# A ranking model on one core: VectorE places fetched rows, ScalarE fetches thirteen fields in one run, and the middle tiles take their rows in six groups

## The reference

```python
x0 = emb[ids].reshape(ids.shape[0], -1)
x = x0
for i in range(cross_w.shape[0]):
    s = x @ cross_w[i]
    x = x0 * s[:, None] + cross_b[i] + x
h = jax.nn.relu(x0 @ w1 + b1)
h = jax.nn.relu(h @ w2 + b2)
h = jax.nn.relu(h @ w3 + b3)
logit = jnp.concatenate([x, h], axis=1) @ out_w + out_b
return jax.nn.sigmoid(logit)
```

## Time and profile before

| | us |
|---|---|
| median of 3 runs (515.51 to 515.76) | 515.7 |
| profiled execution | 515.57 |
| its span, first to last instruction | 513.8 |
| TensorE busy | 478.8 (93%) |
| GpSimd busy | 372.1 (72%) |
| VectorE busy | 247.9 (48%) |
| ScalarE busy | 33.5 (7%) |

### The profile page before, as it was taken

How to read it: one execution, slowest core, us unless ns; L and a number is a source line. 1 busy time by engine, 2 the same in 40 slices (tenths; PEclk the granted TensorE clock), 3 DMA queues, 4 the chain that set the end, 5 groups by cost and what they waited for, 6 DMA issues and landing times.

```text
span 513.8 us, 13128 instructions
## 1 busy us (share of the span) xinstructions
PE 478.8 (93%) x2912; PEld 444.7 (87%) x2912; DVE 247.9 (48%) x490; ACT 33.5 (7%) x68; POOL 372.1 (72%) x400
## 2 busy tenths in 40 slices
PE   2699899998998999899899999999999899999997
PEld 1399798898998889899799989888898889999996
DVE  5776446354363635436264443645454263544335
ACT  4642000000000000000000000000000000000112
POOL 5777777777777777777777777777777777777740
PEclk9999999999999999999899999999999899999999
DMA  7981111111111111111111111111111111111100
GB/s 223 385 300 29 29 28 26 31 27 27 29 29 28 26 32 27 28 30 27 28 28 30 28 28 30 29 26 28 29 28 26 31 28 26 28 29 26 27 18 2
DMA packets 18142, 24.61 MB, mean 48 GB/s; under 512 B 7845, under 2 KB 8832, under 8 KB 18064
## 3 DMA queue, kind: packets, MB, share of 16 engines
q0 software_dynamic: 12576, 12.90, 11.3%
q1 hardware_dynamic: 4154, 9.71, 5.3%
q10 hardware_dynamic: 1334, 1.17, 0.7%
HBM read 24.41 MB, written 0.01 MB: 48 GB/s over the span
## 4 chain that ended last, share of the span: by engine, by line
PE 61%; POOL 18%; issue 11%; DMA 6%; DVE 3%; ACT 0%; POOLq 0%; DVEq 0%
PE l_bank L733 50%; POOL x_raw L345 18%; DMA x_raw<-in_L_rec_emb,idx 6%; PE x_bank L745 4%; PE x_bank L733 2%; PE h_bank L787 2%; DVE x_raw L510 2%; PE l_bank L818 1%; PE h_bank L757 1%; DMA ids<-in_r_ids 1%; PE h_bank L829 0%; PE l_bank L757 0%; DVE xT_lo L534 0%; PE h_bank L733 0%; DVE xT_hi L517 0%
## 5 line engine op out<-in xcount | busy, mean ns | idle before, releaser
L345 POOL DMA_INDIRECT x_raw<-in_L_rec_emb,idx x393 | 371.2, 945 | 122.2 <-issue 107.6
L733 PE MATMUL l_bank<-w_hi,xT_hi 128*128 128x342 f32 (+1 forms) x624 | 144.9, 333 | 0.1
L733 PE MATMUL l_bank<-w_lo,xT_hi 128*128 128x342 f32 (+1 forms) x624 | 138.5, 322 | 0.0
L733 PE MATMUL l_bank<-w_hi,xT_lo 128*128 128x342 f32 (+1 forms) x624 | 138.1, 321 | 0.0
L733 PEld LDWEIGHTS l_bank<-w_lo,xT_hi 128*128 128x128 f32 x624 | 107.3, 191 | 0.0
L733 PEld LDWEIGHTS l_bank<-w_hi,xT_hi 128*128 128x128 f32 x624 | 105.0, 192 | 2.6 <-DVE xT_lo L534 0.4
L733 PEld LDWEIGHTS l_bank<-w_hi,xT_lo 128*128 128x128 f32 x624 | 106.9, 191 | 0.0
L517 DVE CAST xT_hi<-x_bank 128x512 fp32r<-128x512 f32 (+2 forms) x56 | 33.1, 592 | 94.2 <-PE x_bank L745 94.2
L510 DVE COPY_PREDICATED x_raw<-past,x_bank 128x512 f32<-128x512 int32 (+1 forms) x66 | 40.3, 610 | 57.4 <-DMA x_raw<-in_L_rec_emb,idx 56.9
L745 PE MATMUL x_bank<-identity,x_raw 128*128 128x128 f32 x208 | 34.8, 280 | 17.0 <-DVE x_raw L510 16.9
L733 PE MATMUL l_bank<-w_hi,h1T_hi 128*128 128x512 f32 x120 | 48.7, 406 | 0.9 <-DVE h1T_lo L539 0.9
(11 more groups left out here) (97 smaller groups left out, 310.4 us busy)
## 6 DMA issues: line engine op xcount, KB each, us to landing
ids<-in_L_rec_emb SPq DMA_DIRECT2D x1664, 0.2 KB
ids<-in_L_rec_emb ACTq DMA_DIRECT2D x1280, 0.2 KB
w_raw<-in_L_rec_w SPq DMA_DIRECT2D x18, 512.0 KB, 14.6
x_raw<-in_L_rec_emb,idx POOLq DMA_INDIRECT x393, 2.4
b_rows<-in_L_rec_b ACTq DMA_DIRECT2D x1, 512.0 KB
b_rows<-in_L_rec_b ACTq DMA_DIRECT2D x1, 256.0 KB
ids<-in_r_ids SPq DMA_DIRECT2D x1, 208.0 KB, 2.6
b_rows<-in_L_rec_b ACTq DMA_DIRECT2D x1, 128.0 KB
```

Of the source, the lines that this page charges most:

```text
L345: pool.indirect_dma_start(out=dst, out_offset=None, in_=emb, in_offset=rows).then_inc(landed, 16)
L733: done = pe.matmul(bank[:, 0:b - a], x[:, k, :], w[:, k, a:b], start=(k == 0 and n == 0), stop=(k == last_k and n == 2))
```

## The change

- Tiles 1 to 14 take their chunks in six groups of 3, 2, 2, 2, 2 and 2; tile 0 keeps four groups, tile 15 its own six. Counters of groups follow (`seen`).
- VectorE copies the rows that were fetched one by one into place (`place`, ahead of the masked copy of the group that holds fields 20 and 21).
- ScalarE fetches field 20 of thirteen tiles instead of ten (tiles 2, 12 and 15 are new), in one run with loads of 32 addresses: 16 rows ahead of tile 0's last cast, the rest behind it, and all of them ahead of its work for tile 15. It stops only for a free one of its two buffers.
- VectorE takes over the casts of tile 0's first hidden layer, of tile 15's first two groups, and of the second hidden layer of tile 14; the cast and the subtraction of the second hidden layer stand one group later.

```diff
-    SIZES = [4, 3, 4, 2]
+    FIRST_GROUPS = in_groups([4, 3, 4, 2])
+    GROUPS = in_groups([3, 2, 2, 2, 2, 2])
...
-    ACT_TILES = [3, 4, 5, 6, 8, 9, 10, 11, 13, 14]
+    ACT_TILES = [2, 3, 4, 5, 6, 8, 9, 10, 11, 12, 13, 14, 15]
...
-    ACT_SHARES = [24, 28, 24, 28]
+    ACT_FIRST = 16
+    ACT_REGS = 32
...
             def first_step():
...
                     if g == 1:
                         load_rows()
+                    if g == len(FIRST_GROUPS) - 1:
+                        act.wait_ge(sp_idx_ready, 1)
+                        fetch(ACT_FIRST)
                     x_hi(0, g)
-                h1_hi(0)
...
+                fetch(ACT_REGS - ACT_FIRST)
+                while fetched[0] < P * len(ACT_TILES):
+                    fetch(ACT_REGS)
...
             def last_step(t):
-                x_hi(t, 0)
-                h2_hi(t - 1)
-                for g in range(1, len(LAST_GROUPS)):
+                for g in range(2, len(LAST_GROUPS)):
                     x_hi(t, g)
...
+            def place(t, g):
+                if t in SP_TILES and SP_FIELD // FPK in groups(t)[g]:
+                    i = SP_TILES.index(t)
+                    dve.wait_ge(sp_landed[i % SP_BUFS], 16 * P * (i // SP_BUFS + 1))
+                    dve.tensor_copy(x_buf[t % 2][:, SP_FIELD * E:(SP_FIELD + 1) * E], sp_rows[i % SP_BUFS]).then_inc(sp_placed, 1)
+                if t in ACT_TILES and ACT_FIELD // FPK in groups(t)[g]:
+                    j = ACT_TILES.index(t)
+                    dve.wait_ge(act_landed[j % ACT_BUFS], 16 * P * (j // ACT_BUFS + 1))
+                    dve.tensor_copy(x_buf[t % 2][:, ACT_FIELD * E:(ACT_FIELD + 1) * E], act_rows[j % ACT_BUFS]).then_inc(act_placed, 1)
+
             def make_whole(t, g):
+                place(t, g)
```

More of the change, by code:

```diff
@@ L24, in dcn_ranker_kernel, with in_groups @@
     FPK = P // E
-    SIZES = [4, 3, 4, 2]
-    NG = len(SIZES)
-    GROUPS = [list(range(sum(SIZES[:g]), sum(SIZES[:g + 1]))) for g in range(NG)]
-    assert sum(SIZES) == K1
+    def in_groups(sizes):
+        assert sum(sizes) == K1
+        return [list(range(sum(sizes[:g]), sum(sizes[:g + 1]))) for g in range(len(sizes))]
+    FIRST_GROUPS = in_groups([4, 3, 4, 2])
+    GROUPS = in_groups([3, 2, 2, 2, 2, 2])
     LAST_GROUPS = [[0, 1, 2, 3], [4, 5, 6], [7, 8], [12], [9, 10], [11]]
@@ L36, in groups, with seen @@
     def groups(t):
-        return LAST_GROUPS if t == TILES - 1 else GROUPS
-    FIRST = GROUPS[0][-1] * FPK + FPK
+        return LAST_GROUPS if t == TILES - 1 else FIRST_GROUPS if t == 0 else GROUPS
+    def seen(t):
+        return sum(len(groups(u)) for u in range(t))
+    NG = max(len(groups(t)) for t in range(TILES - 1))
+    assert all(len(groups(t)) % 2 == 0 for t in range(TILES))
+    FIRST = FIRST_GROUPS[0][-1] * FPK + FPK
     QUICK = 2
@@ L104, in dcn_ranker_kernel @@
     LO_READ = [5, 10, 13, 17]
-    assert all(HI_AHEAD[g].stop > max(COPIES - 1, GROUPS[g][0] - 1 + COPY_WITH - 1) for g in range(NG))
+    assert all(HI_AHEAD[g].stop > max(COPIES - 1, ks[0] - 1 + COPY_WITH - 1) for g, ks in enumerate(FIRST_GROUPS))
     ctx = ExitStack()
@@ L177, in dcn_ranker_kernel @@
         x_bank = [pb(f"x_bank{i}") for i in range(2)]
-        assert all(len(ks) * P <= 512 - E for t in (0, TILES - 1) for ks in groups(t)[1::2])
+        assert all(len(ks) * P <= 512 - E for t in range(TILES) for ks in groups(t)[1::2])
         end_bank = x_bank[1][:, 512 - E:512]
@@ L327, in _ @@
                     if t >= 2:
-                        read = next(i for i, old in enumerate(GROUPS) if ks[-1] in old)
-                        pool.wait_ge(x_transposed, NG * (t - 2) + read + 1)
+                        read = next(i for i, old in enumerate(groups(t - 2)) if ks[-1] in old)
+                        pool.wait_ge(x_transposed, seen(t - 2) + read + 1)
                     landed = gathered_last[g] if t == TILES - 1 else gathered[t % 2][g]
@@ L431, in first_step @@
             def first_step():
-                for g in range(NG):
+                for g in range(len(FIRST_GROUPS)):
                     for n in HI_AHEAD[g]:
@@ L504, in make_whole @@
                 else:
-                    dve.wait_ge(gathered[t % 2][g], 16 * sum(of_pool(u, f) for u in range(t % 2, t + 1, 2) for f in range(a, a + n)))
+                    dve.wait_ge(gathered[t % 2][g], 16 * sum(of_pool(u, f) for u in range(t % 2, t + 1, 2) if g < len(groups(u))
+                                                             for f in fields(groups(u)[g])))
                 if t in SP_TILES and SP_FIELD in range(a, a + n):
@@ L579, in h1_lo @@
                 for half in range(2):
-                    if t > 0:
-                        h1_hi(t, half)
+                    h1_hi(t, half)
                     dve.wait_ge(h1T_hi_ready, 2 * t + half + 1)
@@ L657, in step @@
                 x_lo(t, 1)
-                h2_hi(t - 1)
-                h2_lo(t - 1)
-                for g in range(2, NG):
+                for g in range(2, len(groups(t))):
                     make_whole(t, g)
@@ L859, in first_step @@
                     copy_hi(n)
-                for g in range(NG):
+                for g in range(len(FIRST_GROUPS)):
                     l1(0, g, BODY, first=True)
-                    if g < NG - 1:
+                    if g < len(FIRST_GROUPS) - 1:
                         transpose_x(0, g + 1)
```

69 lines of the change are left out of this document (22 added, 47 removed).

## The result

The changed kernel takes **537.82 us** (median of 4 runs, 537.20 to 538.73), where the kernel before takes 515.7: a ratio of 1.0431, with a 95% interval of 1.0413 to 1.0449. It is slower by 22.1 us.

A forecast was written before the change was run, and what follows sets the result against it. ScalarE's row fetching was taken to set the end: span 513.8 + 21.9 (cast moved) + 1.5 (clock) = 537.2, plus 1.8 of execution above span, 539.0 us. Its own range was 530 to 548; eight in ten, 513 to 548.

The forecast's parts named there:

- What bounds: ScalarE's queue, though 7% busy, is full: 104 row fetches take 27.74 to 28.45 us in a tile of 30 us.
- Start: ScalarE's first 16 fetches fit its 5.27 us of idle time ahead of tile 0's cast at 46.30.
- Pitch: ScalarE's fetching: 0.215 us a row and 2.1 us a load make 9.05 us for 32 rows, 51 times.
- rival one: ScalarE keeps up, 32 rows in 8.54 us or less, so GpSimd's and the groups' gain stands: 511.6 us; chance 0.16.
- Shift: Cast of tile 15's group 2 moves from 490.6 to 512.5, and everything behind it by 21.9 us.
- Clock: TensorE behind tile 15's wait: clock at 0.50 of full, four chunks take 7.20 us instead of 5.70, 1.5 us more.
- TensorE's arrival: TensorE reaches its wait in tile 15 at about 505, or 507 at a low clock, and waits 5 us or more.
- Where it stalls: TensorE waits several us before the transposes of chunks 9 and 10 in tile 6 and from tile 11 on.
- VectorE: Extra pieces and two placements add 1.4 us per tile on VectorE, hidden with 0.4 us to spare at the tightest place.
- rival three: VectorE becomes the bound if ScalarE keeps up and a placement takes 0.43 us or more; 516.0 at 0.6; chance 0.03.
- The gain that is hidden: Two gathers fewer on GpSimd and smaller groups bring tile 14's last pair of transposes 4.0 us earlier.

## Why the prediction was right

The forecast of 539.0 us stands 1.2 above the median of 537.82 and 0.3 above the profiled execution.

- **What bounds.** That ScalarE's queue was full although it was 7% busy was the reading that decided. It held, and the experiment with twelve fields that fit shows the other side: where ScalarE has the time, GpSimd's gathers set the pace (there up to tile 13) and TensorE runs through to the end behind them. The place of the cast in the queue is worth 3.3 us of the 22.1; without it the landing of the same field would still have held the end.
- **Start.** The cast of tile 0 came at 47.38 and not at 46.30. The first 16 fetches were to lie in ScalarE's idle time; the idle time of 5.27 us ahead of the cast is as before, so they cost nothing there. The cast of tile 0's group 1, ahead of every fetch, is already 1.08 us later (33.35 against 32.27). In the profiled executions of the ten kernels shown here this cast stands between 46.23 and 48.11, without an order by what was changed: the 1.1 us are the difference of single executions.
- **Pitch.** 32 rows take 9.00 us, (511.12 - 52.08) / 51, where 9.05 was forecast: loads of 2.2 us instead of 2.1, rows of 0.212 instead of 0.215. Over 51 loads these 0.05 us make 2.5 us, the largest miss of the sum. SyncE's lower rate, and with it rival one, does not carry over: an issue takes 0.090 us in the median on ScalarE and 0.073 on SyncE, which the trace of before shows as well. What the prediction gave against rival one was weaker than it looked: the four stretches that lie within 0.7 us are four of twelve whole ones, and the twelve go from 26.87 to 28.94; but their mean, 28.1 us, is that of the four. The Trainium skill (DMA: Bandwidth & Descriptors, "Issuing engines are not separate DMA queues") calls the issuing engine's time "usually small relative to the DMA itself". For one row the runs agree, 0.21 us of issuing against 0.8 from there until the rows can be used (511.26 to 512.04 above); for the time they do not, since 1664 issues stand one behind another.
- **Shift.** 20.6 us instead of 21.9, the sum of the two, which have opposite signs.
- **Clock.** 2.5 us instead of 1.5: in proportion the term that was mis-sized most. The row it was taken from the earlier trace rows stood behind a wait of 2.54 us. The wait here was 6.39 us, the low stretch was longer, and more of TensorE's work lay in it. The misses of shift and clock have opposite signs too, so part of the closeness is luck. (The stated bounds of 8.9 and 9.25 us for 32 rows give 531 to 549 by the prediction's own sum, not 530 to 548.)
- **TensorE's arrival.** Forecast 505 to 507 with a wait of 5 us or more; it arrived at 505.97 and waited 6.39. Field 20 of tile 14 was placed at 474.88, forecast 476.3.
- **Where it stalls.** Wrong in part. Tile 6 was right, with 9.32 us; a wait of 1.59 us for field 20 in tile 5 was not forecast, and "from tile 11 on" was too early. Tile 7 takes no field from ScalarE, which gives it back a tile of 30 us, and it loses 6 us with each field after that, so the next stall is a wait of 0.67 us in tile 12, and 7.56 us follow in tile 13. These stalls have no part in the sum, since only the last one counts.
- **VectorE.** The 26 placements took 0.18 and 0.19 us in the median (fields 21 and 20) and 0.20 and 0.21 in the mean, so 0.22 was enough; only one, of 0.43, reached rival three's price. VectorE's busy time grew by 262.8 - 247.9 = 14.9 us; about 3.3 of that are the casts it took over in tiles 0 and 15, which leaves 0.8 in each of 14 tiles, forecast 1.4.
- **The gain that is hidden.** Rival one counted on 4.0 us for two gathers fewer ahead of the end of tile 14 and the groups; no run here has both with ScalarE keeping up, so the 4.0 is not measured. The twelve fields that fit have one gather fewer there: tile 14's last pair comes 3.0 us earlier (463.46 against 466.43), the time falls by 2.5 (ratio 0.9951), and 1.3 of that are the groups. With a step of 1.25 us for the second gather it would be some 3.8, an estimate. GpSimd's last gathers in tile 15 hold the end only where field 20 of that tile is left to them, as in the run with ten fields.

## What to carry to other kernels

Look at the queue of an engine before giving it work, and not at its busy share: DMA issues and register loads are in no busy time, and here 104 issues filled 28 of 30 us. Work that is asked for at one pace and comes at another builds up a delay that appears where a consumer stands behind it in the queue; give each its own rate (36 us a field, 30 us a tile) and spread the requests so that the totals fit at every point. After each gain ask what is late next in the last stage: a tile-14 gain of 1.5 us was worth nothing until tile 15 had one gather fewer.

## What the runs showed of the hardware

In the change the granted clock went to 0.50 around four waits of TensorE's. It did so for 10.2 us each time around those of 9.32, 7.56 and 6.39 us (221.25 to 231.49, 436.29 to 446.53 and 507.97 to 518.21), where it fell while TensorE was still waiting, and for 3.4 us after the one of 2.44 us, where it fell 1.5 us after TensorE had started again (477.25). Before, after 2.54 us, it was also 3.4 us. The length of the wait does not settle it: with loads of 16 the last wait of TensorE's is 7.72 us, and the low stretch around it 6.8 us (530.84 to 537.66).

About two thirds of a fetch's 0.212 us is instructions. The forms of ScalarE's fetches and loads, and of SyncE's issues, as count and duration in ns (min/median/max):

```profile
L394 ACTq MOVE ids<-in_L_rec_emb x1664: 29/29/29, 40.9 to 511.0; - x185
L394 ACTq DMA_DIRECT2D ids<-in_L_rec_emb x1664: 90/90/497, 40.9 to 511.0; - x185
...
L391 ACTq TENSOR_LOAD <-at_bytes x53: 1203/2195/2297, 39.6 to 501.9; - x53
...
L302 SPq DMA_DIRECT2D ids<-in_L_rec_emb x1664: 73/73/325, 26.5 to 454.1; - x185
```

A move takes 0.03 us and most issues 0.09, but 214 of the 1664 take 0.23 to 0.50, so that an issue is 0.117 in the mean. That leaves 0.07 us a row in which no instruction of ScalarE's shows, most of it in pauses of 0.03 between the instructions. Why some issues take longer, and what the pauses are, was not tried; a kernel with fewer bytes in a row or without the moves would tell.
